# Four output buffers, earlier statistics, and a second transpose phase in two parts, in a gated block and quantised feed-forward on eight cores

## The chip, the cores and the metric

One Trainium2 chip; the kernel runs the same program on 8 of its cores, each on 4096 of the 32768 tokens, with all weights. No core talks to another. The metric is the time in microseconds (us) of the slowest core.

## What is computed

Cut from the reference (D = 2048, 4096 inner channels, 5632 hidden channels):

```python
x = x + attn(layernorm(x))      # "attn" is a gated block without attention
x = x + ffn(layernorm(x))

def attn(x):                    # x is its own identity here
    xn = (x - mu) * rsqrt(var + 1e-5) * gamma + beta
    z, gate = split(einsum('bsd,ed->bse', xn, W_in))
    out = z * sigmoid(clip(z)) * softmax(-dt) * silu(clip(gate))
    return einsum('bse,de->bsd', out, W_out) + x

def ffn(x):                     # int32 weights w, W = (w - 128) * scale
    return (silu(x @ Wg.T) * (x @ Wu.T)) @ Wd.T
```

## The kernel before

Each core makes 8 passes (`p`) of 512 tokens, a pass being four chunks (`tc`) of 128 tokens. Pass 0 is longer: beside it the weights are cast to bf16 and the int32 ones converted (VectorE, through `qi` and `qo`), and it is paced by these loads. Weights come from HBM in slabs of 512 KB through seven buffers `wb`, in a fixed order, from SyncE's queue; output stores and input loads are issued by GpSimd, in program order.

The stages of a pass, on TensorE:

1. First transposes (line 325): 16 steps `k` of four 128x128 transposes into one of two PSUM banks (`pb[4 + k % 2]`), each step evicted by ScalarE into `xnT` (line 572).
2. Input projection (line 338), 64 slabs; VectorE and ScalarE make `actb` of each pair.
3. Output projection (line 351) in two halves `P2`, each of 32 slabs for two chunks, which fill all eight PSUM banks: `pb[4..7]` for the even chunk, `pb[0..3]` for the odd one. After each half VectorE computes x2 for its two chunks in four pieces `j` each (lines 496 and 499, by way of `etmp`), then the statistics of both (`ln_stats`, line 503; helper line 441), a chain of some 30 small instructions (Newton steps), and the coefficients for ScalarE (line 515), which writes `xn4` (line 586). The second half's matmuls overwrite banks, so they wait for `x2` of the first half: the even banks for chunk 0, the odd ones for chunk 1 (line 363).
4. Second transposes (line 372), as the first, of all four chunks; evictions at line 591.
5. Gate and up (line 384), 88 slabs, into `actb`.
6. Down projection (line 397) in two halves of 44 slabs, with the banks as in 3. After each half VectorE adds x to the result, piece by piece, into a staging buffer (line 547), and GpSimd stores each piece, 256 KB (line 266), after the fourth piece also issuing the input load of 1 MB for pass p+2 (line 271). The second half's matmuls wait for `fin` of chunks 0 and 1 (line 406), the next pass's transposes for `fin` of chunk 2 (line 322), its input projection for `fin` of chunk 3 (line 337).

Staging is in two of the eight scratch tiles `gsc`, numbers 2 and 6, so piece j waits for the store of piece j − 2 (line 546), and a chunk's first piece for the last stores of the chunk before (line 539). VectorE also waits for the last stores of the pass before the first clip of the next pass (line 475), since `gsc[2]` and `gsc[6]` are scratch there.

All instructions of an engine run in program order. Every matmul and transpose is recorded under the helper's line 316.

Of the kernel before, what the change touches and what calls it, by code (L numbers as in the profile page):

```python
# [15 lines left out]
T = 512  # L16
# [47 lines left out]
def build_program():  # L64
# [27 lines left out]
    with contextlib.ExitStack() as st:  # L92
        def sb(name, shape, dt):
            return st.enter_context(nc.sbuf_tensor(name, shape, dt))
# [4 lines left out]
        etmp = [sb(f"etmp{i}", [128, T], F32) for i in range(2)]  # L99
# [19 lines left out]

        pb = [st.enter_context(nc.psum_tensor(f"pb{i}", [128, T], F32)) for i in range(8)]  # L120

        sem_names = (["t", "v", "s", "g", "cst", "dt1", "dt2", "dt3", "od0", "od1"]
                     + [f"wb{i}" for i in range(NWB)]
                     + [f"qi{i}" for i in range(2)]
                     + [f"qo{i}" for i in range(2)]
# [58 lines left out]
        def gen_gpsimd(E):  # L184
# [76 lines left out]
            for p in range(NP):  # L261
                for tc in range(4):
                    r0 = p * T + tc * 128
                    for j in range(4):
                        u.wait(E, f"fin:{p}:{tc}" if j == 3 else f"finj:{p}:{tc}:{j}")
                        ii = E.dma_start(out_hbm[r0:r0 + 128, j * T:(j + 1) * T],  # L266
                                         gsc[2 + 4 * (j % 2)][:, :]) if E else None
                        u.inc(f"od{j % 2}", 16, f"oD:{p}:{tc}:{j}", ii)
                    if p + 2 < NP:
                        r1 = (p + 2) * T + tc * 128  # L270
                        ii = E.dma_start(xslot(p + 2, tc), x_in[r1:r1 + 128, :]) if E else None
                        u.inc(f"x{4 * (p % 2) + tc}", 16, f"xin:{p + 2}:{tc}", ii)
            if E:
                E.wait_ge(sems["od0"], u.cnt["od0"])
                E.wait_ge(sems["od1"], u.cnt["od1"])

        def gen_sync(E):
            g = 0
# [33 lines left out]
        def gen_tensor(E):  # L312
# [7 lines left out]
            for p in range(NP):  # L320
# [62 lines left out]
                u.wait(E, f"x2:{p}:3")  # L383
                for h in range(NH):
                    if h >= 2:
# [29 lines left out]
        def gen_vector2(E):  # L415
# [51 lines left out]
            for p in range(NP):  # L467
                if p == 0:
                    ln1_block(0)
                for e in range(NZ):  # L470
                    sgg = p * NSLAB + 2 * e + 1
                    u.wait(E, f"su:{sgg}")
                    if p == 0 and e == 0:
                        u.wait(E, "dtwcols")
                    if p > 0 and e == 0:
                        u.wait(E, f"oD:{p - 1}:3:2")
                        u.wait(E, f"oD:{p - 1}:3:3")
                    b = 4 * (e % 2)
                    pz, pg = pb[2 * (e % 2)], pb[2 * (e % 2) + 1]
                    op(lambda pz=pz, b=b: E.tensor_scalar(gsc[b][:, :], pz[:, :], 15.0, -15.0, OP.min, OP.max), f"zc:{p}:{e}")  # L480
# [9 lines left out]
                for P2 in range(2):  # L490
                    last_slab = p * NSLAB + 2 * NZ + (P2 + 1) * NZ - 1
                    u.wait(E, f"su:{last_slab}")
                    for tci in range(2):
                        tc = 2 * P2 + tci
                        for j in range(4):
                            op(lambda p=p, tc=tc, j=j: E.tensor_scalar(etmp[j % 2][:, :], xslot_j(p, tc, j),  # L496
                                                                       coef[:, 8 + tc:9 + tc], coef[:, 12 + tc:13 + tc],
                                                                       OP.mult, OP.add))
                            op(lambda p=p, tc=tc, tci=tci, j=j: E.tensor_tensor(  # L499
                                xslot_j(p, tc, j), etmp[j % 2][:, :],  # L500
                                pb[(4 if tci == 0 else 0) + j][:, :], OP.add),
                                f"x2:{p}:{tc}" if j == 3 else None)
# [30 lines left out]
                for P2 in range(2):  # L533
                    last_slab = p * NSLAB + 4 * NZ + 2 * NH + (P2 + 1) * NH - 1
                    u.wait(E, f"su:{last_slab}")
                    for tci in range(2):
                        tc = 2 * P2 + tci
                        if tc > 0:
                            u.wait(E, f"oD:{p}:{tc - 1}:2")
                            u.wait(E, f"oD:{p}:{tc - 1}:3")  # L540
                        elif p > 0:
                            u.wait(E, f"oD:{p - 1}:3:2")
                            u.wait(E, f"oD:{p - 1}:3:3")
                        for j in range(4):
                            if j >= 2:
                                u.wait(E, f"oD:{p}:{tc}:{j - 2}")
                            op(lambda p=p, tc=tc, tci=tci, j=j: E.tensor_tensor(  # L547
                                gsc[2 + 4 * (j % 2)][:, :], xslot_j(p, tc, j),
                                pb[(4 if tci == 0 else 0) + j][:, :], OP.add),
                                f"fin:{p}:{tc}" if j == 3 else f"finj:{p}:{tc}:{j}")  # L550

        def gen_scalar(E):
# [8 lines left out]
            for p in range(NP):  # L561
# [12 lines left out]
                for e in range(NZ):  # L574
                    if e >= 2:
                        u.wait(E, f"gat:{p}:{e - 2}")
                    b = 4 * (e % 2)
                    u.wait(E, f"zc:{p}:{e}")
                    op(lambda b=b: E.activation(gsc[b + 1][:, :], gsc[b][:, :], AF.Sigmoid), f"sz:{p}:{e}")  # L579
                    u.wait(E, f"gc:{p}:{e}")  # L580
                    op(lambda b=b: E.activation(gsc[b + 3][:, :], gsc[b + 2][:, :], AF.Sigmoid), f"sg2:{p}:{e}")  # L581
                for P2 in range(2):
                    u.wait(E, f"st2:{p}:{P2}")
                    for tci in range(2):
                        tc = 2 * P2 + tci
                        op(lambda p=p, tc=tc: E.activation(xn4[:, tc * D:(tc + 1) * D], xslot(p, tc), AF.Identity,  # L586
                                                           scale=coef[:, 16 + tc:17 + tc], bias=coef[:, 20 + tc:21 + tc]),
                           f"xnf:{p}:{tc}")
# [107 lines left out]
```

## Time and profile before

| | us |
|---|---|
| timed runs | 8210.12 and 9429.92, median 8820.02 |
| profiled execution | 8243.51 |
| its span, slowest core | 8241.9 |
| the other cores' spans | 8182.5 to 8221.2 |
| TensorE busy | 6661.5 |
| VectorE busy | 1993.9 |
| ScalarE busy | 900.5 |

The profile is of one execution, on its slowest core. The span goes from the first to the last instruction, and little lies around it. Busy times are shares of the whole; a wait is put down to the engine and line whose work ended it. The granted clock of TensorE is given in parts of its full speed, 2.4 GHz.

### The profile page before, as it was taken

What the parts mean: (1) busy time and instruction counts of PE and PEld (TensorE: products, weight loads), DVE (VectorE), ACT (ScalarE), POOL (GpSimd) and SP (SyncE); (2) the same over time, 40 slices, a digit from 0 to 9 for tenths busy, and PEclk for the clock granted to TensorE, in tenths of its full rate; (3) what the DMA queues carried; (4) which work ended last, traced back from release to release, by engine and by line L of the source; (5) the groups of instructions that cost most, each with busy time, mean ns of one, the idle gap of its engine ahead of it and who ended that gap; (6) DMA issues with size and microseconds to landing.
All of it is one profiled execution on the core that took longest, in us unless ns stands there. A gap on an engine that the chain in (4) does not pass through costs nothing.

```text
span 8241.9 us, 82175 instructions; the slowest of 8 cores (8182.5 to 8241.9 us)
## 1 busy us (share of the span) xinstructions
PE 6661.5 (81%) x29616; PEld 2988.4 (36%) x30208; DVE 1993.9 (24%) x3488; ACT 900.5 (11%) x1202; POOL 246.2 (3%) x458
## 2 busy tenths in 40 slices
PE   1026645889799998989798998989798979999897
PEld 0012212334344443434343443434343434444343
DVE  1014333214301241115211331114211431124100
ACT  1000000002010111011110101111110201011100
POOL 1001111000000000000000000000000000000000
PEclk8568878899899998989899998989899989999897
DMA  9999889784546654484547563575448454655456
GB/s 146 108 197 305 289 269 302 229 264 156 197 141 209 212 183 154 158 261 151 184 153 234 185 212 125 187 234 171 165 152 266 156 194 143 204 199 188 149 163 203
DMA packets 416524, 1606.80 MB, mean 195 GB/s; under 512 B 46224, under 2 KB 46320, under 8 KB 395008
## 3 DMA queue, kind: packets, MB, share of 16 engines
q1 hardware_dynamic: 350208, 1275.22, 47.1%
q0 software_dynamic: 65920, 326.28, 16.1%
q8 instruction: 250, 4.10, 0.2%
q14 instruction: 146, 1.20, 0.1%
HBM read 1548.87 MB, written 153.11 MB: 207 GB/s over the span
## 4 chain that ended last, share of the span: by engine, by line
PE 72%; DMA 11%; DVE 6%; another core or an unknown queue 6%; issue 3%; ACT 2%; POOL 1%; DVEq 0%; ACTq 0%; POOLq 0%; SPq 0%
PE pb L316 72%; DMA qi<-wqg 3%; DMA qi<-wqd 3%; DMA qi<-wqu 3%; DMA out<-gsc 2%; ACT xnT L572 1%; DVE etmp L496 1%; DVE qo L427 1%; DVE qo L429 1%; DVE bnb L441 1%; DVE xres L499 1%; DVE gsc L547 1%; ACT xnT L591 0%; ACT xn L586 0%
## 5 line engine op out<-in xcount | busy, mean ns | idle before, releaser
L316 PE MATMUL pb<-xnT,wb 128*128 128x512 bf16 x19056 | 4311.7, 387 | 750.2 <-DVE actb L485 542.3
L316 PEld LDWEIGHTS pb<-xnT,wb 128*128 128x128 bf16 x19456 | 1929.2, 99 | 3129.1 <-issue 924.9
L316 PE MATMUL pb<-wb,actb 128*128 128x512 bf16 x9536 | 2200.0, 391 | 330.7 <-DVE gsc L547 154.2
L316 PEld LDWEIGHTS pb<-wb,actb 128*128 128x128 bf16 x9728 | 969.1, 100 | 1560.2 <-issue 536.4
L525 DVE SCALAR_TENSOR_TENSOR actb<-pb,suct,gsc 128x512 bf16<-128x512 f32 x352 | 264.3, 751 | 2188.0 <-PE pb L316 2185.5
L316 PE MATMUL pb<-idmt,xn 128*128 128x128 bf16 x1024 | 151.1, 299 | 474.2 <-ACT xn L586 206.5
L600 ACT ACTIVATE gsc<-pb,sgct 128x512 f32<-128x512 f32 x352 | 241.9, 687 | 2329.1 <-PE pb L316 2329.0
L579 ACT ACTIVATE gsc<-gsc 128x512 f32<-128x512 f32 x256 | 161.5, 631 | 1938.1 <-DVE gsc L480 1938.1
L480 DVE TENSOR_SCALAR gsc<-pb 128x512 f32<-128x512 f32 x256 | 177.2, 692 | 598.5 <-PE pb L316 541.1
L316 PEld LDWEIGHTS pb<-idmt,xn 128*128 128x128 bf16 x1024 | 90.1, 126 | 538.3 <-issue 537.5
L427 DVE TENSOR_SCALAR qo<-qi 128x2048 bf16<-128x2048 int32 x88 | 108.0, 1227 | 696.0 <-DMA qi<-wqg 520.0
L266 POOL DMA_DIRECT2D out<-gsc x128 | 69.4, 542 | 6608.8 <-DVE gsc L547 6591.9
L483 DVE TENSOR_TENSOR gsc<-gsc 128x512 f32<-128x512 f32 x256 | 177.4, 693 | 254.0 <-ACT gsc L581 254.0
L572 ACT ACTIVATE xnT<-pb,bcct,gcct 128x512 bf16<-128x512 f32 x128 | 99.6, 778 | 1028.9 <-PE pb L316 1016.5
L485 DVE SCALAR_TENSOR_TENSOR actb<-gsc,dtwt 128x512 bf16<-128x512 f32 x256 | 192.3, 751 | 26.9 <-DVE gsc L484 0.5
L547 DVE TENSOR_TENSOR gsc<-xres,pb 128x512 f32<-128x512 f32 x64 | 44.0, 688 | 611.7 <-PE pb L316 494.6
L481 DVE TENSOR_SCALAR gsc<-pb 128x512 f32<-128x512 f32 x256 | 177.1, 692 | 29.6 <-DVE gsc L480 3.2
L484 DVE TENSOR_TENSOR gsc<-pb,gsc 128x512 f32<-128x512 f32 x256 | 177.1, 692 | 26.6
L581 ACT ACTIVATE gsc<-gsc 128x512 f32<-128x512 f32 x256 | 161.5, 631 | 45.3 <-DVE gsc L481 44.4
L429 DVE SCALAR_TENSOR_TENSOR qo<-qi,sdbt 128x2048 bf16<-128x2048 int32 x44 | 100.9, 2293 | 185.8 <-DMA qi<-wqd 185.6
L496 DVE TENSOR_SCALAR etmp<-xres,coef 128x512 f32<-128x512 f32 x64 | 35.0, 546 | 354.8 <-PE pb L316 348.6
L547 DVE TENSOR_TENSOR gsc<-qi,pb 128x512 f32<-128x512 f32 x32 | 22.0, 688 | 381.9 <-PE pb L316 328.0
(75 smaller groups left out, 933.3 us busy)
## 6 DMA issues: line engine op xcount, KB each, us to landing
wb<-wd_s SPq DMA_DIRECT2D x704, 512.0 KB, 5.2
wb<-win_s SPq DMA_DIRECT2D x512, 512.0 KB, 3.7
wb<-wout_s SPq DMA_DIRECT2D x512, 512.0 KB, 5.2
wb<-wg_s SPq DMA_DIRECT2D x352, 512.0 KB, 3.5
wb<-wu_s SPq DMA_DIRECT2D x352, 512.0 KB, 3.5
qi<-wqg POOLq DMA_DIRECT2D x44, 1024.0 KB, 11.1
qi<-wqu POOLq DMA_DIRECT2D x44, 1024.0 KB, 10.8
qi<-wqd POOLq DMA_DIRECT2D x44, 1024.0 KB, 10.0
```

The source lines that it names most:

```text
L316: i = E.matmul(out_ap, lhsT, rhs, start=start, stop=stop) if E else None
L427: op(lambda i_=i_: E.tensor_single_scalar(qo[i_ % 2][:, :], qi[i_ % 2][:, :], -128.0, OP.add), f"wqts:{i_}")
L429: op(lambda i_=i_: E.scalar_tensor_tensor(qo[i_ % 2][:, :], qi[i_ % 2][:, :], -128.0, sdbt[:, :], OP.add, OP.mult), f"wqts:{i_}")
L480: op(lambda pz=pz, b=b: E.tensor_scalar(gsc[b][:, :], pz[:, :], 15.0, -15.0, OP.min, OP.max), f"zc:{p}:{e}")
L481: op(lambda pg=pg, b=b: E.tensor_scalar(gsc[b + 2][:, :], pg[:, :], 15.0, -15.0, OP.min, OP.max), f"gc:{p}:{e}")
L483: op(lambda b=b: E.tensor_tensor(gsc[b][:, :], gsc[b + 2][:, :], gsc[b + 3][:, :], OP.mult))
L484: op(lambda pz=pz, b=b: E.tensor_tensor(gsc[b + 2][:, :], pz[:, :], gsc[b + 1][:, :], OP.mult))
L485: op(lambda b=b, e=e: E.scalar_tensor_tensor(actb[:, e * T:(e + 1) * T], gsc[b + 2][:, :], dtwt[:, e:e + 1], gsc[b][:, :], OP.mult, OP.mul ...
L525: op(lambda h=h: E.scalar_tensor_tensor(actb[:, h * T:(h + 1) * T], pb[2 * (h % 2) + 1][:, :], suct[:, h:h + 1], gsc[4 * (h % 2)][:, :], O ...
L572: op(lambda k=k: E.activation(xnT[:, k * T:(k + 1) * T], pb[4 + k % 2][:, :], AF.Identity, scale=gcct[:, k:k + 1], bias=bcct[:, k:k + 1]), ...
L579: op(lambda b=b: E.activation(gsc[b + 1][:, :], gsc[b][:, :], AF.Sigmoid), f"sz:{p}:{e}")
L600: op(lambda h=h: E.activation(gsc[4 * (h % 2)][:, :], pb[2 * (h % 2)][:, :], AF.Silu, scale=sgct[:, h:h + 1]), f"sil:{p}:{h}")
```

## The change

- Output staging uses four buffers, `gsc[1]`, `[3]`, `[5]`, `[7]`, one per piece, with a semaphore each; piece j of a chunk waits for the store of piece j of the chunk before.
- Since ScalarE writes these four tiles in the input projection, the wait for the last stores of a pass goes from VectorE's first clip to ScalarE's first sigmoid.
- `etmp` is gone; x2 goes by way of `gsc[0]` and `gsc[4]`.
- The statistics of a chunk stand right after its x2, before the x2 of the next chunk.
- The second transposes are done in two parts: A for chunks 0 and 1, B for chunks 2 and 3, each of 16 steps of two transposes and an eviction of 256 columns. ScalarE's order is: `xn` of chunks 0 and 1, evictions A, `xn` of chunks 2 and 3, evictions B.

```diff
@@ gpsimd: stores
-                                         gsc[2 + 4 * (j % 2)][:, :]) if E else None
-                        u.inc(f"od{j % 2}", 16, f"oD:{p}:{tc}:{j}", ii)
+                                         gsc[2 * j + 1][:, :]) if E else None
+                        u.inc(f"od{j}", 16, f"oD:{p}:{tc}:{j}", ii)
@@ tensor: second transposes
                 for k in range(ND):
                     if k >= 2:
-                        u.wait(E, f"T2ev:{p}:{k - 2}")
-                    for tc in range(4):
+                        u.wait(E, f"T2evA:{p}:{k - 2}")
+                    for tc in range(2):
                         if k == 0:
                             u.wait(E, f"xnf:{p}:{tc}")
                         mm(pb[4 + k % 2][:, tc * 128:(tc + 1) * 128],
                            xn4[:, tc * D + k * 128: tc * D + (k + 1) * 128] if E else None,
                            idmt[:, :] if E else None, True, True,
-                           inc_label=(f"T2mm:{p}:{k}" if tc == 3 else None))
-                u.wait(E, f"T2ev:{p}:{ND - 1}")
+                           inc_label=(f"T2Amm:{p}:{k}" if tc == 1 else None))
+                u.wait(E, f"T2evA:{p}:{ND - 1}")
+                for k in range(ND):
+                    if k >= 2:
+                        u.wait(E, f"T2evB:{p}:{k - 2}")
+                    for tc in range(2, 4):
+                        if k == 0:
+                            u.wait(E, f"xnf:{p}:{tc}")
...
+                           inc_label=(f"T2Bmm:{p}:{k}" if tc == 3 else None))
+                u.wait(E, f"T2evB:{p}:{ND - 1}")
                 u.wait(E, f"x2:{p}:3")
@@ vector: first clip of a pass
-                    if p > 0 and e == 0:
-                        u.wait(E, f"oD:{p - 1}:3:2")
-                        u.wait(E, f"oD:{p - 1}:3:3")
@@ vector: x2 and statistics
                     for tci in range(2):
                         tc = 2 * P2 + tci
                         for j in range(4):
-                            op(lambda p=p, tc=tc, j=j: E.tensor_scalar(etmp[j % 2][:, :], xslot_j(p, tc, j),
+                            op(lambda p=p, tc=tc, j=j: E.tensor_scalar(gsc[4 * (j % 2)][:, :], xslot_j(p, tc, j),
...
                                 f"x2:{p}:{tc}" if j == 3 else None)
-                    for tci in range(2):
-                        tc = 2 * P2 + tci
                         ln_stats(p, tc, 8)
@@ vector: output additions
-                        if tc > 0:
-                            u.wait(E, f"oD:{p}:{tc - 1}:2")
-                            u.wait(E, f"oD:{p}:{tc - 1}:3")
-                        elif p > 0:
-                            u.wait(E, f"oD:{p - 1}:3:2")
-                            u.wait(E, f"oD:{p - 1}:3:3")
                         for j in range(4):
-                            if j >= 2:
-                                u.wait(E, f"oD:{p}:{tc}:{j - 2}")
+                            if tc > 0:
+                                u.wait(E, f"oD:{p}:{tc - 1}:{j}")
+                            elif p > 0:
+                                u.wait(E, f"oD:{p - 1}:3:{j}")
                             op(lambda p=p, tc=tc, tci=tci, j=j: E.tensor_tensor(
-                                gsc[2 + 4 * (j % 2)][:, :], xslot_j(p, tc, j),
+                                gsc[2 * j + 1][:, :], xslot_j(p, tc, j),
@@ scalar
                 for e in range(NZ):
+                    if e == 0 and p > 0:
+                        for jj in range(4):
+                            u.wait(E, f"oD:{p - 1}:3:{jj}")
...
-                for P2 in range(2):
-                    u.wait(E, f"st2:{p}:{P2}")
...
+                u.wait(E, f"st2:{p}:0")
+                for tc in range(2):
+                    op(lambda p=p, tc=tc: E.activation(xn4[:, tc * D:(tc + 1) * D], xslot(p, tc), AF.Identity,
...
                 for k in range(ND):
-                    u.wait(E, f"T2mm:{p}:{k}")
-                    op(lambda k=k: E.activation(xnT[:, k * T:(k + 1) * T], pb[4 + k % 2][:, :], AF.Identity),
-                       f"T2ev:{p}:{k}")
+                    u.wait(E, f"T2Amm:{p}:{k}")
+                    op(lambda k=k: E.activation(xnT[:, k * T:k * T + 256], pb[4 + k % 2][:, 0:256], AF.Identity),
+                       f"T2evA:{p}:{k}")
+                u.wait(E, f"st2:{p}:1")
+                for tc in range(2, 4):
...
+                for k in range(ND):
+                    u.wait(E, f"T2Bmm:{p}:{k}")
+                    op(lambda k=k: E.activation(xnT[:, k * T + 256:(k + 1) * T], pb[4 + k % 2][:, 256:512], AF.Identity),
+                       f"T2evB:{p}:{k}")
```

## Rows read from the trace of the kernel before

**Rows 1.** Page, part 1: busy us, share of span, count.

```profile
PE 6661.5 (81%) x29616; PEld 2988.4 (36%) x30208; DVE 1993.9 (24%) x3488; ACT 900.5 (11%) x1202; POOL 246.2 (3%) x458
```

**Rows 2.** Waits of PE, whole span: total us, times, longest us.

```profile
PE pb L316 <- DVE gsc L547: 213.1, 23, 13.3
PE pb L316 <- ACT xn L586: 206.5, 16, 24.2
```

**Rows 3.** Page, part 5: matmuls by group; idle before them, ended by.

```profile
L316 PE MATMUL pb<-wb,actb 128*128 128x512 bf16 x9536 | 2200.0, 391 | 330.7 <-DVE gsc L547 154.2
```

**Rows 4.** Groups by shape, whole span: transposes, evictions, activation passes.

```profile
L316 PE MATMUL pb<-idmt,xn 128*128 128x128 bf16 x1024 | 151.1, 299 | 474.2 <-ACT xn L586 206.5 <-ACT xn L565 92.0 <-DVE gsc L547 58.9
...
L572 ACT ACTIVATE xnT<-pb,bcct,gcct 128x512 bf16<-128x512 f32 x128 | 99.6, 778 | 1028.9 <-PE pb L316 1016.5 <-ACT xnT L572 1.6
L591 ACT ACTIVATE xnT<-pb 128x512 bf16<-128x512 f32 x128 | 76.4, 597 | 22.3 <-PE pb L316 15.7 <-ACT xnT L591 0.7
L586 ACT ACTIVATE xn<-xres,coef 128x2048 bf16<-128x2048 f32 x16 | 33.5, 2094 | 657.7 <-DVE coef L515 656.6 <-ACT xn L586 0.4
```

**Rows 5.** Timeline, pass 3, between the down halves: start us, us, instruction.

```profile
4473.27 1.48 DVE L547 TENSOR_TENSOR gsc<-xb,pb 128x512 f32<-128x512 f32 x2 [46.31 <-PE pb L316]
4474.52 0.55 POOL L266 DMA_DIRECT2D out<-gsc  x1 [788.18 <-DVE gsc L547]
4479.15 1.48 DVE L547 TENSOR_TENSOR gsc<-xb,pb 128x512 f32<-128x512 f32 x2 [4.40 <-DMA out<-gsc]
...
4480.78 1.86 PE L316 MATMUL pb<-wb,actb 128*128 128x512 bf16 x4 [7.82 <-DVE gsc L547]
...
4493.48 1.48 DVE L547 TENSOR_TENSOR gsc<-xb,pb 128x512 f32<-128x512 f32 x2 [4.95 <-DMA out<-gsc]
4495.11 15.18 PE L316 MATMUL pb<-wb,actb 128*128 128x512 bf16 x57 [12.47 <-DVE gsc L547]
```

**Rows 6.** Timeline, end of pass 3.

```profile
4573.19 1.48 DVE L547 TENSOR_TENSOR gsc<-qi,pb 128x512 f32<-128x512 f32 x2 [78.23 <-PE pb L316]
...
4581.58 1.07 PE L316 MATMUL pb<-idmt,xn 128*128 128x128 bf16 x8 [8.70 <-DVE gsc L547]
```

**Rows 7.** Timeline of DVE, end of the last pass.

```profile
8216.92 1.48 DVE L547 TENSOR_TENSOR gsc<-qi,pb 128x512 f32<-128x512 f32 x2 [94.16 <-PE pb L316]
...
8231.21 0.69 DVE L547 TENSOR_TENSOR gsc<-qi,pb 128x512 f32<-128x512 f32 x1 [0.17 <-DMA out<-gsc]
```

**Rows 8.** Timeline, pass 4, between the output-projection halves: PE, then DVE.

```profile
4889.11 1.87 PE L316 MATMUL pb<-wb,actb 128*128 128x512 bf16 x4 [6.00 <-DVE xres L499]
4895.26 5.08 PE L316 MATMUL pb<-wb,actb 128*128 128x512 bf16 x13 [4.28 <-DVE xres L499]
...
4895.21 3.09 DVE L441 BATCH_NORM_STATS2 bnb<-xres 128x6 f32<-128x512 f32 x4
4898.40 0.26 DVE L442 BATCH_NORM_AGGREGATE mvb<-bnb 128x2 f32<-128x24 f32 x1
```

**Rows 9.** Timeline of ACT, pass 4, before gate and up.

```profile
4979.97 4.28 ACT L586 ACTIVATE xn<-xres,coef 128x2048 bf16<-128x2048 f32 x2 [64.17 <-DVE coef L515]
4984.81 1.29 ACT L591 ACTIVATE xnT<-pb 128x512 bf16<-128x512 f32 x2 [0.56 <-PE pb L316]
4986.29 1.29 ACT L591 ACTIVATE xnT<-pb 128x512 bf16<-128x512 f32 x2 [0.19 <-PE pb L316]
```

**Rows 10.** Timeline of PE, pass 0.

```profile
1223.70 25.86 PE L316 MATMUL pb<-xnT,wb 128*128 128x512 bf16 x110 [46.92 <-DMA wb<-wu_s]
```

**Rows 11.** Windows: length us, PE busy us, clock, DMA share, GB/s.

```profile
4473.00:4477.00 4.00, 0.00 (x0) 0.91 0.97 381
4481.00:4485.00 4.00, 1.64 (x4) 0.50 1.00 158
4540.00:4573.00 33.00, 32.72 (x150) 1.00 0.91 301
```

**Rows 12.** Page, part 3: the software DMA queue: packets, MB, share of 16 engines.

```profile
q0 software_dynamic: 65920, 326.28, 16.1%
```

More of the change, by code:

```diff
@@ L98, in build_program @@
         xb3 = sb("xb3", [128, D], F32)
-        etmp = [sb(f"etmp{i}", [128, T], F32) for i in range(2)]
         xn4 = sb("xn4", [128, 4 * D], BF16)
@@ L120, in build_program @@
         pb = [st.enter_context(nc.psum_tensor(f"pb{i}", [128, T], F32)) for i in range(8)]
-        sem_names = (["t", "v", "s", "g", "cst", "dt1", "dt2", "dt3", "od0", "od1"]
+        sem_names = (["t", "v", "s", "g", "cst", "dt1", "dt2", "dt3", "od0", "od1", "od2", "od3"]
                      + [f"wb{i}" for i in range(NWB)]
@@ L273, in gen_gpsimd @@
             if E:
-                E.wait_ge(sems["od0"], u.cnt["od0"])
-                E.wait_ge(sems["od1"], u.cnt["od1"])
+                for jj in range(4):
+                    E.wait_ge(sems[f"od{jj}"], u.cnt[f"od{jj}"])
         def gen_sync(E):
@@ L380, in gen_tensor @@
                            idmt[:, :] if E else None, True, True,
-                           inc_label=(f"T2mm:{p}:{k}" if tc == 3 else None))
-                u.wait(E, f"T2ev:{p}:{ND - 1}")
+                           inc_label=(f"T2Amm:{p}:{k}" if tc == 1 else None))
[6 more added lines that the diff above has]
+                            u.wait(E, f"xnf:{p}:{tc}")
+                        mm(pb[4 + k % 2][:, tc * 128:(tc + 1) * 128],
+                           xn4[:, tc * D + k * 128: tc * D + (k + 1) * 128] if E else None,
+                           idmt[:, :] if E else None, True, True,
+                           inc_label=(f"T2Bmm:{p}:{k}" if tc == 3 else None))
+                u.wait(E, f"T2evB:{p}:{ND - 1}")
                 u.wait(E, f"x2:{p}:3")
@@ L499, in gen_vector2 @@
                             op(lambda p=p, tc=tc, tci=tci, j=j: E.tensor_tensor(
-                                xslot_j(p, tc, j), etmp[j % 2][:, :],
+                                xslot_j(p, tc, j), gsc[4 * (j % 2)][:, :],
                                 pb[(4 if tci == 0 else 0) + j][:, :], OP.add),
                                 f"x2:{p}:{tc}" if j == 3 else None)
-                    for tci in range(2):
-                        tc = 2 * P2 + tci
                         ln_stats(p, tc, 8)
@@ L574, in gen_scalar @@
                 for e in range(NZ):
+                    if e == 0 and p > 0:
+                        for jj in range(4):
+                            u.wait(E, f"oD:{p - 1}:3:{jj}")
                     if e >= 2:
@@ L581, in gen_scalar @@
                     op(lambda b=b: E.activation(gsc[b + 3][:, :], gsc[b + 2][:, :], AF.Sigmoid), f"sg2:{p}:{e}")
-                for P2 in range(2):
-                    u.wait(E, f"st2:{p}:{P2}")
[L584 to L588, printed above, removed]
-                for k in range(ND):
-                    u.wait(E, f"T2mm:{p}:{k}")
-                    op(lambda k=k: E.activation(xnT[:, k * T:(k + 1) * T], pb[4 + k % 2][:, :], AF.Identity),
-                       f"T2ev:{p}:{k}")
+                u.wait(E, f"st2:{p}:0")
+                for tc in range(2):
+                    op(lambda p=p, tc=tc: E.activation(xn4[:, tc * D:(tc + 1) * D], xslot(p, tc), AF.Identity,
+                                                       scale=coef[:, 16 + tc:17 + tc], bias=coef[:, 20 + tc:21 + tc]),
+                       f"xnf:{p}:{tc}")
+                for k in range(ND):
+                    u.wait(E, f"T2Amm:{p}:{k}")
[3 more added lines that the diff above has]
+                for tc in range(2, 4):
+                    op(lambda p=p, tc=tc: E.activation(xn4[:, tc * D:(tc + 1) * D], xslot(p, tc), AF.Identity,
+                                                       scale=coef[:, 16 + tc:17 + tc], bias=coef[:, 20 + tc:21 + tc]),
+                       f"xnf:{p}:{tc}")
+                for k in range(ND):
+                    u.wait(E, f"T2Bmm:{p}:{k}")
+                    op(lambda k=k: E.activation(xnT[:, k * T + 256:(k + 1) * T], pb[4 + k % 2][:, 256:512], AF.Identity),
+                       f"T2evB:{p}:{k}")
                 for h in range(NH):
```

## The prediction

> **What bounds the kernel now.** I read the page's busy table first. TensorE is busy for 6661.5 us, 81% of the 8241.9 us span [rows 1]; no other engine is near it, so time can only be won where TensorE stands still or where its clock is low. The waits of TensorE then say who stops it. In the passes after the first, two names carry most of it: VectorE's output additions (`gsc`, 213.1 us) and ScalarE's second normalisation (`xn`, 206.5 us) [rows 2]. The groups by shape split the first of them: 154.2 us lie before matmuls that read `actb` (the down projection; 8 boundaries between its halves, 19.3 us each) [rows 3] and 58.9 us before transposes (7 pass ends, 8.4 us each) [rows 4]. These are the places that the change touches, so the rest of the reading is timelines there.
>
> **Part A, output staging, between the down halves.** VectorE adds two pieces, then stands until a store has landed, four times over: it starts at 4473.27 and begins its last pair at 4493.48, so it ends at 4494.96, 21.7 us later, and TensorE idles 7.82 and 12.47 us around four matmuls of 1.86 us [rows 5]. The store is issued 1.25 us after the first addition begins, and the addition that needs its buffer starts 5.9 us after that same beginning [rows 5]. With four buffers the first token chunk needs no store: four additions at the pitch of a pair (1.48 us for two with the gap between, so about 0.80 each) are done 3.1 us after the start. The second chunk's addition j waits only for the first chunk's store j, issued 1.25 + 0.8j us after the start. I let the first land after about 6.3 us (the 5.9 of the row, a little more for four stores in flight) and the others at the pitch of their issue: the last addition starts near 8.9 and ends at 9.7. TensorE's idle is then 0.3 (its last matmul to the first addition) + 9.7 + 0.1 − 1.9 = 8.2 us instead of 19.3: 11.1 saved, times 8, 89 us. Bounds: no wait beyond the row's first one (end at 5.9 + 3.1 = 9.0, saving 11.8 each, 94); or the third and fourth store land a whole round after the first two (5.9 + 5.9 + 1.5 = 13.3, saving 7.5, 60).
>
> The Trainium skill speaks of the same term ("DMA: Bandwidth & Descriptors", section "Anatomy of one DMA — SWDGE (gpsimd) path"): a fixed part of about 2.0 us plus bytes over 436 GB/s. For 256 KB that is an estimate of 2.6 us per store, so by the page the last addition would end near 7.0 and the part would bring 110 us. The row's first store was away 4.5 us until it was seen, in a stretch where the weight stream still ran at 381 GB/s with a DMA share of 0.97 [rows 5, 11]; I keep the row.
>
> **Part B, the pass end.** The first transposes of the next pass need the third chunk's additions. They start now 8.39 us after the additions began (4573.19 to 4581.58) [rows 6]; with four buffers 3.1 + 0.2 us. That is 5.1 in this pass; against the mean of 8.4 us idle per pass end [rows 4], the new idle is 0.3 + 3.1 + 0.2 = 3.6, so 4.8 saved, times 7: 34 us. The fourth chunk then ends at 9.7, well inside the 15 us of transposes (16 evictions at 0.778 us and their gaps [rows 4]). The wait on these stores that moves from VectorE to ScalarE's first sigmoid stands behind these evictions and a whole first pair of slabs. It costs nothing; its price without that cover would be one store, about 4.5 us a pass. The very end: the last addition starts 14.3 us after the first (8216.92 to 8231.21) [rows 7]. There the stores have no weight stream beside them. I put it at 7: 7 us saved once.
>
> **Part C, statistics moved up.** Between the output-projection halves, the second chunk's result now comes after the first chunk's four statistics (3.09 us) and their aggregate (0.26) [rows 8]: with the gaps 3.56 us later. TensorE already waits there for exactly this result (4.28 us, ending at 4895.26 [rows 8]), and nothing else is late, so the delay is paid in full: +3.56 × 7 = +25 us. The same sum of VectorE work is done before the coefficients, so ScalarE's pass is not moved. In pass 0 it costs nothing, because 46.92 us of waiting for the first `wu_s` slab follow [rows 10] and take it up. If that cover were gone it would be 3.6 more.
>
> **Part D, transposes in two parts.** The first half (A) runs while VectorE computes x2 and statistics of the last two chunks. It can begin when the accumulator banks are read, and TensorE's longest wait for `xn` from there on is 24.2 us [rows 2], some 22 of it before ScalarE gets its next coefficients; even at the present pace of 0.74 us per step it needs 12. Behind the second pair of `xn` passes (4.28 us from 4979.97) today 8 pairs of evictions run at 1.48 us each [rows 9]. That cycle is one eviction 0.61, four transposes 0.60, and two hand-overs of 0.14. For 256 columns an eviction comes from two rows with the same operands: (2094 − 778) / 1536 = 0.86 ns per column, so 597 − 219 = 378 ns [rows 4]. The cycle becomes 0.38 + 0.30 + 0.28 = 0.96, which ScalarE alone (2 × 0.46) allows. 7 × 0.52 and 0.4 for the last pair: 4.1 us saved, times 7 passes, 29 us. Bounds: a half costs as much as a whole (cycle 1.36: 0.8 each, 6 us), or just half of it (0.30: cycle 0.88; 4.8 each, 34 us). Pass 0 gains nothing, for the reason in C. The extra instructions (16 evictions a pass) lie in half A, beside VectorE's chain. The replacement of `etmp` by two idle `gsc` buffers costs nothing: same engine, same shape, same order.
>
> **The sum.** −89 − 34 − 7 + 25 − 29 = −134 us. The profiled execution took 8243.5 us, so 8109.5; the lower of the two timed runs, 8210.1, gives 8076, and their median, 8820.0, is the mean of two far-apart numbers and fits neither the span nor the profile. I forecast between the two sums, 8093 us, 1.6% below the mean of the two bases (8226.8).
>
> **Rivals.**
> *It is more than 2%.* In the first 4 us of the idle stretch the granted clock still has a mean of 0.91, so it is at the upper level (2.4 GHz) for nearly all of them; at 4481 it is 0.50, the lower one (1.2 GHz) [rows 11]. The new first gap, 3.6 us, ends within these 4 us. If the clock outlives it, the four matmuls take about 0.9 instead of 1.86 us, and if it outlives the second, of 4.6 us, the start at the lower level goes as well: the first 13 recorded matmuls after such a wait take 5.08 us, 0.39 each, against 32.72 / 150 = 0.22 at clock 1.00 [rows 8, 11], some 2.3 us more. Up to 3.3 × 8 = 26 us. With the stores at their better bound: −134 − 26 − 5 = −165, 8079 from the profiled time, 8045 from the lower run. For it: the gaps get shorter than those after which these rows show the lower level (7.82 and 6.00 us [rows 5, 8]). Against it: the two idle stretches lie close together, with only four matmuls between them.
>
> *It is half.* Stores come a round later and the half evictions are not cheaper: −60 − 34 − 7 + 25 − 6 = −82, 8161 us. For it: the wait before the last pair, 4.95 us with an input load in the same queue, is as long as the first, 4.40 [rows 5].
>
> *The weight stream starves TensorE.* Steady down work takes 0.91 of the DMA engines at 301 GB/s, and a window with an input load shows 1.00 at only 158 GB/s [rows 11]. The software queue as a whole moved 326.28 MB in 16.1% of the span, 246 GB/s [rows 12]. Now 2 MB of stores and 2 MB of input loads come within some 12 us instead of 24: 4 MB at 158 to 246 GB/s are 17 to 26 us of DMA time, of which about 5 are done when TensorE starts again. It has seven slabs of 1.73 us, 12 us, in hand. If the queue takes everything first, TensorE stands 0 to 8 us per boundary; 3 us would make 8093 into 8117. This is also the rival on the other side: it decides from 134 / 8 = 17 us of starvation per boundary, and at 38 us per boundary the kernel is 2% slower, 8093 + 8 × 38 = 8397. Against it: TensorE shows no wait on `wd_s` now, and fair sharing leaves the stream half of the engines.
>
> *It does nothing.* A, B and D would have to turn into other waits altogether; C alone gives 8243.5 + 25 = 8268. Little speaks for that, since VectorE has no other work in those stretches.
>
> **How the numbers follow.** Likeliest (the sum within its bounds) 0.50; more than 2% 0.20; half 0.13; starvation of a few us 0.10; slower by over 2% 0.04; nothing or C alone 0.03. Two per cent is about what a measurement of this kernel can tell from no change, and it is 165 us here, 31 from my sum; so 0.06 of the likeliest goes to faster: faster 0.26, within 2% 0.70, slower 0.04. The range: from 8030 (the lower base with the first rival, and some 15 below) to 8175 (half, with something for starvation). The likeliest alone lies in 8060 to 8140.
>
> **What would show it.** In the changed profile the `gsc` additions should stand four together, with one wait on `out<-gsc` of about 3 us per boundary; TensorE's idle before `actb` matmuls released by `gsc` should be near 65 us in all (154.2 now), before transposes near 25 (58.9). The second wait on `xres` between the output halves should be 7.8 us, not 4.28. Evictions of 256 columns should last 0.38 us and the stretch from the second `xn` pass to the first gate matmul should shrink by 4. A wait on `wd_s` right after the down halves' boundary would show the starvation. The forecast is wrong if the stores of one chunk land one by one a full wait apart, or if a shorter gap leaves a new clock penalty.

## The result: 1.3% faster

| | before | changed |
|---|---|---|
| profiled execution, us | 8243.51 | 8106.17 |
| span of the slowest core, us | 8241.9 | 8104.6 |
| ratio of the timed runs | | 0.9869, 95% interval 0.9836 to 0.9902 |

The ratio leaves out runs that the chip disturbed; what is compared lies at 8210 and 8216 us before and from 8094 to 8132 us changed, and the median of 8820.02 us shown ahead of the prediction is no base for it. A later measurement of the changed kernel gave 0.9856 (0.9832 to 0.988).

The page of the changed kernel, its busy table and its group of down and output matmuls (line 315 is now the helper's); beside [rows 1, 3]:

```profile
PE 6643.1 (82%) x29616; PEld 2970.6 (37%) x30208; DVE 1993.8 (25%) x3488; ACT 922.4 (11%) x1330; POOL 246.2 (3%) x458
...
L315 PE MATMUL pb<-wb,actb 128*128 128x512 bf16 x9536 | 2170.6, 388 | 288.4 <-DVE gsc L548 81.1
```

Its waits of TensorE (total us, times, longest us), beside [rows 2]:

```profile
PE pb L315 <- ACT xn L597: 142.6, 16, 16.1
PE pb L315 <- DVE gsc L548: 106.0, 23, 8.5
...
PE pb L315 <- DMA wb<-wu_s: 56.9, 1, 56.9
```

Its transposes and its half evictions (busy us, mean ns, idle before), beside [rows 4]:

```profile
L315 PE MATMUL pb<-idmt,xn 128*128 128x128 bf16 x1024 | 168.1, 292 | 390.2 <-ACT xn L597 142.6 <-ACT xn L566 92.7 <-ACT xnT L573 36.0
...
L602 ACT ACTIVATE xnT<-pb 128x256 bf16<-128x256 f32 x128 | 49.2, 384 | 21.7 <-PE pb L315 15.4 <-ACT xnT L602 0.4
```

The output additions now hold TensorE for 106.0 us instead of 213.1, and of these 81.1 instead of 154.2 between the down halves; ScalarE's `xn` holds it for 142.6 instead of 206.5. Busy time hardly moved (6661.5 to 6643.1), as it should.

The boundary of the down halves in pass 3, changed kernel, slowest core (start us, length us, instruction, idle before and its releaser), beside [rows 5]:

```profile
4440.06 3.06 DVE L548 TENSOR_TENSOR gsc<-xb,pb 128x512 f32<-128x512 f32 x4 [46.25 <-PE pb L315]
4448.60 0.69 DVE L548 TENSOR_TENSOR gsc<-xb,pb 128x512 f32<-128x512 f32 x1 [5.47 <-DMA out<-gsc]
4449.61 2.27 DVE L548 TENSOR_TENSOR gsc<-xb,pb 128x512 f32<-128x512 f32 x3 [0.33 <-DMA out<-gsc]
...
4443.27 1.86 PE L315 MATMUL pb<-wb,actb 128*128 128x512 bf16 x4 [3.46 <-DVE gsc L548]
4452.03 18.25 PE L315 MATMUL pb<-wb,actb 128*128 128x512 bf16 x72 [6.89 <-DVE gsc L548]
```

Four additions stand together, then one wait of 5.47 us and four more: 11.8 us from first to last instead of 21.7. The same boundary on core 3 of the same run:

```profile
4410.24 3.06 DVE L548 TENSOR_TENSOR gsc<-xb,pb 128x512 f32<-128x512 f32 x4 [46.25 <-PE pb L315]
...
4413.45 1.86 PE L315 MATMUL pb<-wb,actb 128*128 128x512 bf16 x4 [3.45 <-DVE gsc L548]
4414.39 0.54 POOL L270 DMA_DIRECT2D xb<-x  x1
4416.39 3.06 DVE L548 TENSOR_TENSOR gsc<-xb,pb 128x512 f32<-128x512 f32 x4 [3.09 <-DMA out<-gsc]
...
4419.60 5.77 PE L315 MATMUL pb<-wb,actb 128*128 128x512 bf16 x17 [4.29 <-DVE gsc L548]
```

Here the wait is 3.09 us and the whole takes 9.2. Over the whole run of core 3 the additions hold TensorE between the down halves for 64.6 us:

```profile
L315 PE MATMUL pb<-wb,actb 128*128 128x512 bf16 x9728 | 2180.5, 387 | 261.2 <-DVE gsc L548 64.6 <-DVE xb L506 54.6 <-DVE xres L506 54.6
```

In the timeline above, the input load goes out at 4414.39, 4.15 us after the first addition began. This difference between cores comes back below.

Between the output-projection halves, pass 4, TensorE of the changed kernel, beside [rows 8]:

```profile
4838.77 1.87 PE L315 MATMUL pb<-wb,actb 128*128 128x512 bf16 x4 [6.01 <-DVE xres L506]
4848.46 56.65 PE L315 MATMUL pb<-wb,actb 128*128 128x512 bf16 x247 [7.83 <-DVE xres L506]
```

The second wait is 7.83 us where it was 4.28. Before gate and up, same pass: ScalarE's second pair of `xn` passes, two pairs of half evictions, and TensorE's first gate matmuls, beside [rows 9]:

```profile
4933.16 4.28 ACT L597 ACTIVATE xn<-xres,coef 128x2048 bf16<-128x2048 f32 x2 [13.18 <-DVE coef L520]
4938.00 0.86 ACT L602 ACTIVATE xnT<-pb 128x256 bf16<-128x256 f32 x2 [0.56 <-PE pb L315]
4939.05 0.86 ACT L602 ACTIVATE xnT<-pb 128x256 bf16<-128x256 f32 x2 [0.19 <-PE pb L315]
...
4946.96 33.38 PE L315 MATMUL pb<-xnT,wb 128*128 128x512 bf16 x141 [1.27 <-ACT xnT L602]
```

From 4933.16 to 4946.96 are 13.8 us. In the kernel before, the same stretch begins at 4979.97 [rows 9] and ends with

```profile
4997.18 13.10 PE L316 MATMUL pb<-xnT,wb 128*128 128x512 bf16 x49 [1.48 <-ACT xnT L591]
```

so it was 17.2 us.

**How much of the 137 us is the change.** The steadiest measure is the pitch: from the first output addition of pass 1 to that of pass 6, over 5. On core 0 it fell from 905.9 ((7190.28 − 2660.67) / 5) to 890.9 ((7112.68 − 2658.40) / 5); over all eight cores its mean fell from 904.5 to 889.3, 15.2 a pass. The core 0 of the profile before had something else besides. The windows of its last stages, and of core 3's, show (length us, TensorE busy us, clock, DMA share, GB/s):

```profile
core 0: us, PE busy (x), PEclk, DMA share, GB/s
8024.00:8190.00 166.00, 148.40 (x552) 0.78 0.76 238
core 3: us, PE busy (x), PEclk, DMA share, GB/s
8024.00:8190.00 166.00, 118.36 (x537) 0.88 0.67 223
```

Nearly as many recorded matmuls (552 and 537) kept core 0 busy for 148.4 us and core 3 for 118.4: its clock was at 0.78 in a dense stretch. In the difference of the two profiles this and the stretch around it are some 31 us: the last full pass became shorter by 27.1 where 15.1 is the rule, and from the last boundary to the end 32.6 us went on core 0 and 13.1 on core 3. Pass 0 went the other way, 11 us longer on core 0 (the first addition at 1754.58 and 1765.54) but 24 shorter on core 4 (1761.6 and 1737.4); it is paced by the int32 loads, and the same point lies anywhere between 1720 and 1766 us over the cores of the profiles of both kernels and of e1, e2, e3, e5, e7, e8, e10 and e12. Without both, −137 − 11 + 31 = −117 us, near the 108 us of the ratio (0.0131 × 8213).

### The profile page after: what moved, and what is told of

Its sections match the earlier page's. It is cut to its first block, busy times and chain, and to the rows that moved or that the text cites. A ratio compares the mean times of both kernels' runs of the same rounds, so it can differ in the third digit from the quotient of the medians.

```text
span 8104.6 us, 82695 instructions; the slowest of 8 cores (8052.4 to 8104.6 us)
## 1 busy us (share of the span) xinstructions
PE 6643.1 (82%) x29616; PEld 2970.6 (37%) x30208; DVE 1993.8 (25%) x3488; ACT 922.4 (11%) x1330; POOL 246.2 (3%) x458
## 4 chain that ended last, share of the span: by engine, by line
PE 73%; DMA 10%; DVE 6%; another core or an unknown queue 6%; issue 2%; ACT 2%; POOL 1%; DVEq 0%; ACTq 0%; POOLq 0%; SPq 0%
PE pb L315 73%; DMA qi<-wqg 3%; DMA qi<-wqd 3%; DMA qi<-wqu 3%; ACT xnT L573 1%; DVE gsc L503 1%; DVE bnb L451 1%; DMA out<-gsc 1%; DVE qo L437 1%; DVE qo L439 1%; DVE xres L506 1%; DVE gsc L548 1%; ACT xn L597 0%; ACT xnT L602 0%
## 5 line engine op out<-in xcount | busy, mean ns | idle before, releaser
L315 PE MATMUL pb<-wb,actb 128*128 128x512 bf16 x9536 | 2170.6, 388 | 288.4 <-DVE gsc L548 81.1
L315 PE MATMUL pb<-idmt,xn 128*128 128x128 bf16 x1024 | 168.1, 292 | 390.2 <-ACT xn L597 142.6
L503 DVE TENSOR_SCALAR gsc<-xres,coef 128x512 f32<-128x512 f32 x64 | 34.9, 546 | 362.9 <-PE pb L315 356.3
## 6 DMA issues: line engine op xcount, KB each, us to landing
qi<-wqg POOLq DMA_DIRECT2D x44, 1024.0 KB, 11.2
qi<-wqd POOLq DMA_DIRECT2D x44, 1024.0 KB, 10.2
```

The costliest lines, as they stand in the source:

```text
L315: i = E.matmul(out_ap, lhsT, rhs, start=start, stop=stop) if E else None
```

## Experiments

All are judged by the pitch, as a mean of the eight cores where no other is said. Its scatter between two runs of one kernel is small: 889.3 and 888.9 in the two runs of the changed one. Times are the lowest of their timed runs; the kernel before lay at 8195 to 8215 us beside them. Where no ratio is given, none was measured. e5 to e9 and e11 start from the kernel of e4, with the statistics back.

**e1: the buffers alone.**

```diff
-gsc[2 + 4 * (j % 2)], semaphores od0, od1, wait for piece j - 2
+gsc[2 * j + 1], semaphores od0 to od3, wait for piece j of the chunk before
```

> The kernel before with the four output buffers alone (parts A and B). Measure: the distance between the first output additions of pass 1 and pass 6, over 5, on the slowest core: 905.9 us before, 890.9 changed. If the parts add up, it is 905.9 - 9.2 (between the down halves) - 4.8 (pass end) = 891.9, and the whole run is 8 x 9.2 + 7 x 4.8 + 5.7 at the end = 113 us shorter than before. Rival, the weight stream gives part of it back after each boundary: a wait on wd_s shows and the pitch stays above 895.

Measured: 8092 us, ratio 0.9838 (0.9707 to 0.997), mean pitch 889.3; on the slowest core 891.5, where 891.9 was expected. TensorE's waits, slowest core:

```profile
PE pb L316 <- ACT xn L582: 206.3, 16, 24.0
...
PE pb L316 <- DVE gsc L540: 106.6, 23, 10.5
```

All of the whole change's 15.2 us a pass is in the buffers; nothing on `wd_s` shows among these waits. On cores 0 and 2 there are 3.4 and 6.2 us of it in all, so the rival is small and not quite absent. The wait for `xn` is as before (206.3).

**e2: the statistics alone.**

```diff
                                 f"x2:{p}:{tc}" if j == 3 else None)
-                    for tci in range(2):
-                        tc = 2 * P2 + tci
                         ln_stats(p, tc, 8)
```

> The kernel before with the statistics moved alone (part C). Adding up: TensorE's second wait for x2 between the output-projection halves is 7.8 us instead of 4.3, pitch 905.9 + 3.6 = 909.5, the whole 25 us slower than before. Rival, the move pays for itself because the coefficients come earlier: pitch 905.9 or less.

Measured: 8221 us, ratio 1.0 (0.99 to 1.01), mean pitch 907.9, that is +3.4 where +3.6 was expected. The group of matmuls that waits between the output-projection halves, slowest core:

```profile
L316 PE MATMUL pb<-wb,actb 128*128 128x512 bf16 x9728 | 2181.7, 388 | 353.6 <-DVE gsc L545 155.6 <-DVE xres L499 55.0 <-DVE xb L499 54.6
```

`xres` and `xb` hold it for 55.0 + 54.6 us, against 40.4 + 40.4 before, 28.8 more: 3.6 at each of 8 boundaries. The rival, a pitch of 905.9 or less, is out. The ratio cannot tell 0.3%; the pitch and the waits do.

**e3: the split transposes alone.**

```diff
-16 x (4 transposes, evict 512 columns)                 after xn of all chunks
+16 x (2 transposes, evict 256 columns)  chunks 0, 1    beside VectorE's x2 and statistics
+16 x (2 transposes, evict 256 columns)  chunks 2, 3    after their xn
```

> The kernel before with the second transposes in two parts alone (part D). Adding up: from the second pair of xn passes to the first gate matmul 13.8 us instead of 17.2, pitch 905.9 - 3.4 = 902.5, the whole 24 us faster than before. Rival, the work of half A gets in the way of VectorE (PSUM or SBUF) and delays the coefficients: the xn passes start later than 27.9 us after the first x2 operation of the half, and the pitch stays near 905.

Measured: 8195 us, mean pitch 900.5, −4.0. TensorE's waits, slowest core:

```profile
PE pb L316 <- DVE gsc L558: 213.6, 23, 14.8
PE pb L316 <- ACT xn L604: 142.8, 16, 16.4
```

The output additions hold TensorE as before (213.6), `xn` less by 64 us, 8 a pass. Half A now fills most of that time with transposes, and 4.0 a pass are won. The rival is out by both of its signs: in this run the second pair of `xn` passes starts 27.8 to 27.9 us after the half's first x2 operation in passes 1 to 6, as in the kernel before.

**e4 and e10: the changed kernel with the statistics back.** One kernel, run twice; the pitch is from e10.

```diff
-                        ln_stats(p, tc, 8)
+                    for tci in range(2):
+                        tc = 2 * P2 + tci
+                        ln_stats(p, tc, 8)
```

> The changed kernel with the statistics back behind both x2. Adding up: pitch 890.9 - 3.6 = 887.3 and 25 us faster than the changed kernel, about 135 us faster than before by timed runs. Rival, the order matters only with etmp and not with the split: no difference to the changed kernel, 890.9.

> The same kernel as e4, beside the two others on one chip: 8065 us and a pitch of 884 to 887.5 on every core, 25 us faster than the changed kernel. If the pitch is as in the changed kernel (888 to 891), the order of the statistics did nothing.

Measured: 8065 and 8055 us, e4's ratio 0.9803 (0.9715 to 0.9892); mean pitch in e10 885.5. The parts add up: −15.1 (e1) − 4.0 (e3) = −19.1 beside −19.0 here, and with +3.4 (e2) −15.7 beside −15.2 for the whole. So the statistics cost what the split brings, and the change as made is worth its buffers.

**e5: the input loads later.**

```diff
-after each chunk's 4 stores: its input load
+after the second chunk's 4 stores: the input loads of both
```

> The changed kernel with the statistics back, and the input loads of a pair of chunks issued behind the second chunk's stores instead of one load behind each chunk's. Where passes 6 and 7 have no input load, the second chunk's last addition ends 9.2 to 9.4 us after the first one's start; in passes 0 to 5 it is 11.6 to 13.4. If the input load in the same queue is what holds the first chunk's stores back, it ends near 9.3 in all passes and the pitch falls by 2.5 from 886 to 883.5. If the stores are held back by the weight stream instead, the time stays near 11.8 and the pitch at 886.

Measured: 8069 us, mean pitch 886.5. On core 0 the second chunk's last addition in passes 1 to 5 ends 9.9 to 11.1 us after the first one's start, against 11.4 to 13.0 in e10: some of the hold came from the load, not all. But the pitch on core 0 is 887.46, and it was 887.47; the mean of the eight cores rose by 1.0. So neither expectation came true as it stands. TensorE's waits, slowest core:

```profile
PE pb L316 <- DVE gsc L551: 98.8, 23, 7.8
...
PE pb L316 <- DMA wb<-wd_s: 5.4, 9, 1.0
```

A wait on `wd_s` is among them with 5.4 us. It is on all eight cores of this run (1.6 to 6.8 us), while in the runs above only some cores have it, none of them the slowest. On core 0 the additions won 1.8 us a pass (means of 10.4 and 12.2) and the pass nothing: part may have come back as this wait, and the last section looks at the rest.

**e6 and e7: eight buffers, loads as before and late.**

```diff
-gsc[2 * j + 1]
+gsc[2 * j + 1 - tc % 2]        # odd chunks in the even tiles, semaphores od0 to od7
```

> The changed kernel with the statistics back and eight staging buffers (even chunks in the odd ones, odd chunks in the even ones), so that no addition between the down halves waits for a store. The eight additions end 6.3 us after they begin; TensorE resumes 5.4 us earlier than with four: pitch 886 - 5.4 = 880.6, whole 8 x 5.2 = 42 us faster than with four buffers, near 8025. Rival, starvation: stores, input loads and weight slabs now meet within 6 us and TensorE waits for wd_s after the boundary, 3 us or more: pitch above 883.

> Eight buffers and the input loads of a pair behind the second chunk's stores. With no addition waiting for a store the place of the loads should matter no more: as with eight buffers alone, 880.6. If starvation is there, loading later shifts it and changes the pitch by over 1.

Measured: in e6 cores 0 to 3 have spans of 8028.0 to 8030.4 us and a mean pitch of 886.1, where 880.6 was expected; e7 8033 us and 884.1. The additions do end 6.2 us after they begin, on all cores and in all passes but the last (6.6). TensorE's waits in e6, core 0:

```profile
PE pb L315 <- DVE gsc L553: 64.1, 23, 3.8
...
PE pb L315 <- DMA wb<-wd_s: 17.0, 10, 3.1
```

`gsc` fell from 105 to 64 us, and 17.0 us of `wd_s` appeared. One boundary in e6 (TensorE's timeline, then two windows with the clock in the third column):

```profile
4388.09 1.86 PE L315 MATMUL pb<-wb,actb 128*128 128x512 bf16 x4 [3.45 <-DVE gsc L553]
4391.25 14.85 PE L315 MATMUL pb<-wb,actb 128*128 128x512 bf16 x60 [1.30 <-DVE gsc L553]
4409.25 5.98 PE L315 MATMUL pb<-wb,actb 128*128 128x512 bf16 x21 [3.14 <-DMA wb<-wd_s]
...
4406.90:4410.90 4.00, 1.65 (x4) 0.70 0.96 306
4410.90:4414.90 4.00, 4.00 (x18) 0.88 1.00 341
```

TensorE resumes 6.4 us after the additions began (4384.9 to 4391.25; 12.0 in the changed kernel's rows above), works 14.85 us through the slabs it has in hand, and then stands 3.14 us for `wd_s`. The clock falls in this stretch (0.70, then 0.88), so the first matmuls after it are slow as well. This is the starvation rival of the prediction. The changed kernel has at most 1.1 us of it on a core, in all its passes; the next shortening of the boundary brings it.

**e8, e9 and e11: input loads in the next pass's input projection.** e8 and e11 are one kernel with eight buffers, e9 has four.

```diff
-                    if p + 2 < NP:                # behind the stores of chunk tc
+                if p + 2 < NP:                    # behind all stores of pass p
+                    for tc in range(4):
+                        u.wait(E, f"gat:{p + 1}:{8 + 4 * tc}")
                         ... dma_start(xslot(p + 2, tc), x_in[r1:r1 + 128, :])
```

> Eight buffers, statistics back, and all input loads of a pass issued during the next pass's input projection (behind gat 8, 12, 16, 20), where the DMA engines are half idle. With eight buffers and the loads at the boundary, one pass in two showed a wait for wd_s of about 3 us and lasted 887.4 instead of 884; the passes without input loads lasted 880.5. If the input loads are what starves the weight stream and holds the stores, no wait for wd_s is left and all passes last 880.5: pitch 5.5 below the 886 of eight buffers, whole about 30 us faster, near 8000. Rival, the stores alone suffice for it: wd_s waits of about 17 us in all remain and the pitch stays at 884 to 886.

> Four buffers, statistics back, input loads in the next pass's input projection. If the input load holds the stores, the second chunk's last addition ends 9.2 to 9.5 us after the first one's start in every pass and on every core, all passes last 883.9 (that of the last full pass with four buffers) instead of 887.4, and the difference between the two cores of a pair is gone. Rival, the cores of a pair disturb each other through the weight stream: the later core still needs over 10.5.

> The same kernel as e8 (eight buffers, statistics back, loads in the next pass), for its ratio. 8012 us against 8205 before: ratio 0.976. All passes at 880.6 us on every core; a spread over cores or passes would mean that the evenness of e8 was chance.

Measured, eight buffers: 8011 and 8014 us, ratio 0.979 (0.9756 to 0.9825) in e11, so this is faster than the kernel before and than the changed one (8079 us in e12, measured beside e11); whether by more than 2% against the kernel before, the interval leaves open. TensorE's waits in e8, slowest core:

```profile
PE pb L317 <- DVE gsc L555: 64.1, 23, 3.8
PE pb L317 <- DMA wb<-wout_s: 28.9, 16, 3.5
```

No wait on `wd_s` is left on any core. The pitch is 880.61 to 880.64 on all eight cores of e8 and on cores 4 to 7 of e11. The first and the last of the full passes, e8, core 4:

```profile
2626.20:3506.70 880.50, 816.26 (x3702) 0.95 0.56 191
7029.30:7909.80 880.50, 816.46 (x3702) 0.95 0.55 187
```

Measured, four buffers: 8034 us; cores 0 to 3 have pitches of 884.0, 884.0, 884.8 and 884.0, and in passes 1 to 5 their additions between the down halves end after 8.8 to 10.6 us. With the input loads away from the boundary the stores are hardly held (e9) and the starvation is gone (e8), so both needed the loads there.

**e12: the changed kernel again, for the pairs of cores.**

> The changed kernel itself, beside e11, for its ratio on the same chip and a second look at its passes: 8095 us, ratio 0.986. In each pair of cores (0 and 1, 2 and 3, and so on) the core that comes to the boundary between the down halves later should have the longer pass again, by 2 to 3 us; if the longer one is the earlier, or the same core whatever its order, the link to the order is chance.

Measured: 8079 us, ratio 0.9856, pitches 890.9 and 887.5 on cores 0 and 1, 890.2 and 887.5 on 2 and 3, 890.2 and 887.5 on 4 and 5, 890.2 and 887.5 on 6 and 7. In each pair the longer one is the core that reached pass 1's boundary later (2631.0 and 2621.6 on 0 and 1; 2633.1 and 2619.9 on 6 and 7). In the profile of the first run core 7 was later than core 6 (2642.9 and 2631.4) and it had the longer pitch (890.2 and 887.5). One pass on core 0, then one on core 1, e12:

```profile
3521.70:4412.60 890.90, 817.48 (x3702) 0.94 0.56 189
...
3509.00:4396.40 887.40, 820.80 (x3776) 0.95 0.56 190
```

In e1 cores 3 and 5 are the later ones of their pairs and have the longer pitch (891.5 and 890.2 against 888.8 and 887.5); its cores 0 and 1 are the exception, with 889.5 both (core 0, the earlier one, has 3.4 us of waits on `wd_s`). So it goes with the order and not with the core's number. With the input loads away from the boundary the difference is gone in e8, and in e9 all but gone (884.8 against 884.0 on one pair). In e5 no input load of a core's own goes out before its second chunk's stores, and the later cores still wait longer for the first store: on core 0 the fifth addition starts 6.8 to 7.6 us after the first one in passes 1 to 5, on core 1 5.4 to 6.3. That the later core's stores meet the earlier one's input load in a memory or a path that the pair shares fits all this, but no run here looked at that path.

## Why the prediction was right, and where it was not

- **The sum.** −134 us was forecast, −1.6% with its base; the change is worth 108 to 117 us, −1.3%. That the two profiles differ by 137 is luck: some 31 of it was a low clock on core 0 before, and pass 0 went 11 the other way. The mechanism and the signs of all parts held, and so did the sizes of B, C and the end. What failed is the size of two terms, of part A above all and of part D. With what was measured on the slowest core in their place the sum is −73 − 34 − 7 + 25 − 24 = −113. The base hid it: 8226.8, a mean of the profile with this low clock and one timed run, lies 14 us above the 8213 of the compared runs, so that 8093 us still lies near the timed 8094 to 8132.
- **Part A, 11.1 us a boundary: the step that failed.** 154.2 − 81.1 = 73.1 us, 9.1 each on the slowest core. The mis-sized step is "I let the first land after about 6.3 us": it was 8.5 on core 0 (4448.60 − 4440.06), from 7.3 to 10.4 in its passes with input loads and 6.3 and 6.1 in the two without. On core 3 the second chunk ends at 9.2 to 10.2, the 9.7 of the forecast, and the wait of 64.6 us is the forecast's 65; on core 0 it ends at 11.6 to 13.4 with input loads and at 9.3 and 9.2 without. In passes 1 to 5 the mean is 9.6 to 9.8 on the earlier core of each pair (1, 3, 5, 6) and 11.2 to 12.2 on the later one. So the step holds for a core that comes first, and the time is set by one that does not. It took one wait for a pair of stores and counted the other stores, but not the input load, which now goes out 4.15 us after the first addition, right behind four stores that nobody waits between; nor did it ask what the pair's other core sends (e5, e12). The trace before had a sign of it. The third pair waited for stores with an input load right behind them, 6.43 us against the 4.40 of the row that was used:

```profile
4487.06 1.48 DVE L547 TENSOR_TENSOR gsc<-xb,pb 128x512 f32<-128x512 f32 x2 [6.43 <-DMA out<-gsc]
```

  (VectorE stood three times between its four pairs there, not four.) With the loads elsewhere (e9) the end is at 8.8 to 10.6 in passes 1 to 5 on cores 0 to 3.
- **The page's rule in part A** (the Trainium skill, "DMA: Bandwidth & Descriptors", section "Anatomy of one DMA — SWDGE (gpsimd) path") gave an estimate of 2.6 us for a store. The nearest to it is the very last boundary, without weight stream and loads: the first addition begins at 8086.93, its store goes out 1.25 later, the buffer is free at 8091.14, 3.0 us. Under load it was 4.6 before [rows 5] and 7.2 on core 0 now, and the row was the better choice.
- **Part B, 4.8 us.** 58.9 − 24.9 = 34.0 us before transposes (106.0 − 81.1 = 24.9): as forecast. **The end**, 7 us: from the third chunk's first addition to the end of the span 25.0 us before (8216.92 to 8241.9) and 17.7 changed (8086.93 to 8104.6), 7.3.
- **Part C, +3.56 us.** 7.83 in place of 4.28, +3.55, and +3.4 in the pitch by e2. In pass 0 TensorE waited at the boundary too (54.6 is for 8 passes), but a wait for `wu_s` of 56.9 us follows there. That it takes the delay up, as forecast, is not shown: pass 0 differs by more than 3.5 us between cores and between runs of one kernel.
- **Part D, 4.1 us.** 17.2 to 13.8: 3.4. The half eviction is 384 ns, where 378 was worked out; the cycle is 1.05 us (4938.00 to 4939.05), not 0.96. The mis-sized term is the two transposes, taken as half of 0.60: the cycle of 1.05 less 0.38 and the 0.28 of the hand-overs leaves 0.39 for two, not 0.30. The bound of 1.36 for a half that costs as much as a whole does not follow from its own terms, which give 0.6 + 0.3 + 0.28, about 1.2; nothing rested on it.
- **Faster by more than 2%** rested on the clock outliving a gap of 3.6 us. It did not: after 3.46 us the four matmuls took 1.86 us, 0.47 each, on both cores shown, as after the longer gap of before [rows 5], and the granted clock from 4443.2 to 4447.2 was 0.50.
- **Starvation** had 0.10 and hardly came in the changed kernel (at most 1.1 us on a core), but it came in e5, e6 and e7, up to 3.1 us at a boundary and 17.0 us in all on core 0 of e6. So its working was sound in kind and its place was one change further on.

## What to carry to other kernels

When a stage boundary is shortened, look at what the same queue issues right behind the transfers that it waits for: here the input loads were moved from the down projection, where the DMA engines are 0.91 busy [rows 11], into the input projection, where the kernel before had them 0.45 busy (4600 to 4700 us). That gave another 21 us with four buffers (e10 to e9, 8055 to 8034) and 22 with eight (e7 to e8, 8033 to 8011, not measured beside each other). Price each reordering by what already waits for the delayed result; the statistics looked neutral on VectorE and took back all that the split won. And judge small parts by a pitch between like points inside the run and on all cores, not by whole times or by the slowest core alone.

## What the runs showed of the hardware that was not expected

The pass lengths stand on a ladder. In the changed kernel and those built on it, nearly all full passes of the cores compared lie within 0.5 us of 880.6, 884.0, 887.5 or 890.8 us, though the additions between the down halves, for one, end anywhere from under 9 to over 13 us after they begin in the kernels with four buffers. Most passes of the kernel before, of e2 and of e3 lie near 898, 901, 904.5 or 908 us. Two passes of e6 on core 0 (length, TensorE busy, clock), and one pass of e10 on core 0 and one on core 1:

```profile
3500.80:4384.90 884.10, 821.15 (x3776) 0.95 0.57 191
4384.90:5272.20 887.30, 824.65 (x3776) 0.95 0.57 190
```

```profile
3515.30:4402.90 887.60, 821.04 (x3776) 0.95 0.56 190
...
3508.80:4393.00 884.20, 820.72 (x3776) 0.95 0.58 191
```

In e6 the second pass holds less idle time than the first (62.6 and 63.0 us) and is 3.2 us longer: the time is in busy matmuls. The same stretch of both passes, the first half of the output projection behind the same wait, e6:

```profile
3834.33 56.24 PE L315 MATMUL pb<-wb,actb 128*128 128x512 bf16 x252 [4.24 <-DVE actb L495]
...
4720.55 57.18 PE L315 MATMUL pb<-wb,actb 128*128 128x512 bf16 x252 [4.24 <-DVE actb L495]
```

252 recorded matmuls of one shape took 56.24 us once and 57.18 the other time. Stretches of 4 us right behind the two waits, clock in the third column:

```profile
3834.30:3838.30 4.00, 3.97 (x11) 0.59 0.37 125
3838.30:3842.30 4.00, 4.00 (x20) 0.98 0.55 176
...
4720.50:4724.50 4.00, 3.95 (x10) 0.50 0.25 76
4724.50:4728.50 4.00, 4.00 (x17) 0.82 0.52 182
```

After the same 4.24 us of waiting the clock stood at its lower level, 1.2 GHz, for most of the first stretch in the one pass (0.59, then 0.98) and for all of it and part of the next in the other (0.50, then 0.82): by these shares some 3.4 us at the lower level against 5.4. The 2.0 us more at half speed cost 1.0, and 57.18 − 56.24 is 0.94. That such differences, summed over the waits of a pass, decide which step of the ladder a pass stands on is argued from this one pair and not shown. It fits that e5 won 1.8 us in the additions of a pass on core 0 and no time, and that all full passes of e8 stand on the lowest step, on every core. What sets the steps was not tested.
